# Four high tiles for staging, two running-sum tiles with separate carries, logits behind the next rows' transposes, and epsilon as a third column

## The reference, cut to what matters

```python
# x (8, 2048, 512)
h = layernorm(x) * (1 + ca) + sa
xn = layernorm(h) * ln_gamma + ln_beta
k, v, r = xn @ Wk.T, xn @ Wv.T, xn @ Wr.T
kv = k * v
csum = cumsum(kv * sigmoid(time_decay) ** t, axis=time)        # over 2048 rows of a batch
wkv = sigmoid(time_first) * kv + sigmoid(time_decay) * shifted(csum)
x = x + ga * ((sigmoid(r) * wkv) @ Wo.T)
h = layernorm(x) * (1 + cb) + sb
# two groups of 32 experts, the best 2 of each group for every row
logits = h @ router_w                     # (rows, 64)
x = x + gb * mean over the two groups of the weighted SwiGLU experts of h
```

## Time and profile before

| | |
|---|---|
| median of the runs | 4927.58 us (3 runs, 4915.73 to 4927.71) |
| the profiled execution | 4905.73 us, its span 4904.0 us |
| share of the span busy | PE 93%, PEld 77%, DVE 63%, ACT 34%, POOL 58% |
| mean granted TensorE clock | 0.971 |
| stage A in the trace | from about 78 to about 1905 us |

### The profile page before, as it was taken

One profiled execution on the slowest core, in us unless ns is written; L12 is line 12 of the kernel. 1 busy time (PEld: TensorE's weight loads), 2 busy tenths in 40 slices (PEclk: granted clock), 3 DMA queues, 4 the chain that ended last, 5 costly groups with the idle time before them and its releaser, 6 DMA issues.

```text
span 4904.0 us, 89177 instructions
## 1 busy us (share of the span) xinstructions
PE 4580.8 (93%) x22649; PEld 3764.6 (77%) x22649; DVE 3080.2 (63%) x6077; ACT 1651.2 (34%) x4093; POOL 2858.1 (58%) x2300
## 2 busy tenths in 40 slices
PE   6999999999999995889999998999999999999998
PEld 4877777777777774667777777888788888888887
DVE  5999999999999996444444444444344444444443
ACT  2444444444444442222222222332222222222222
POOL 2577777777777776445444454555455555555554
PEclk8999999999999997899999999999999999999999
DMA  6767666666666674889899989998998988988887
GB/s 240 234 200 228 195 222 196 214 200 220 207 200 227 196 226 159 261 271 285 252 279 280 280 238 270 294 278 223 290 239 222 260 221 242 258 231 221 220 222 195
DMA packets 434624, 1152.46 MB, mean 235 GB/s; under 512 B 59361, under 2 KB 59362, under 8 KB 415666
## 3 DMA queue, kind: packets, MB, share of 16 engines
q0 software_dynamic: 182512, 454.27, 39.3%
q1 hardware_dynamic: 231106, 619.79, 36.6%
q10 hardware_dynamic: 20736, 75.51, 4.2%
HBM read 719.35 MB, written 463.57 MB: 241 GB/s over the span
## 4 chain that ended last, share of the span: by engine, by line
PE 42%; DMA 12%; issue 4%; POOL 2%; DVE 1%; POOLq 0%; SPq 0%; ACT 0%; DVEq 0%
PE ps L1316 12%; PE ps L1318 12%; PE ps L1317 12%; DMA out<-c_yo,c_idx 11%; PE ps L1325 4%; PE ps L1344 2%; POOL out L1307 1%; POOL c_xg L1274 1%; DMA c_wt<-wsp_d 0%; POOLq L1299 0%; DVE c_yo L1571 0%; POOL list_d L1279 0%; DMA list_d<-pairs,sidx 0%; DMA c_lists<-list_d,c_rowu 0%; DVE c_xl L1559 0%
## 5 line engine op out<-in xcount | busy, mean ns | idle before, releaser
L1307 POOL DMA_INDIRECT out<-c_yo,c_idx x576 | 915.1, 1589 | 933.9 <-DMA out<-c_yo,c_idx 512.5
L1316 PE MATMUL ps<-c_wt,c_xh 128*128 128x512 f32 x2304 | 964.1, 418 | 24.9 <-issue 16.8
L1318 PE MATMUL ps<-c_wt,c_xl 128*128 128x512 f32 x2304 | 910.3, 395 | 0.0
L1317 PE MATMUL ps<-c_wt,c_xh 128*128 128x512 f32 x2304 | 904.0, 392 | 0.0
L1274 POOL DMA_INDIRECT c_xg<-h2g_d,c_idx x576 | 565.0, 981 | 507.6 <-DVE c_yo L1571 400.5
L1555 DVE TENSOR_TENSOR c_hh<-ps,c_sil 128x256 f32<-128x256 f32 x576 | 244.2, 424 | 913.5 <-ACT c_sil L1398 843.5
L1571 DVE SCALAR_TENSOR_TENSOR c_yo<-ps,c_wc,c_xg 128x512 f32<-128x512 f32 x576 | 432.3, 750 | 529.2 <-PE ps L1318 261.5
L442 PE MATMUL ps<-xTh,wTh 128*128 128x512 f32 x1536 | 625.9, 407 | 53.5 <-DVE xTl L818 46.9
L1403 ACT CAST c_xh<-ps 128x512 fp32r<-128x512 f32 x576 | 339.2, 589 | 962.2 <-PE ps L1325 874.2
L709 POOL DMA_INDIRECT list_d<-pairs,sidx x496 | 545.5, 1100 | 188.5 <-issue 123.9
L1398 ACT ACTIVATE c_sil<-ps 128x256 f32<-128x256 f32 x576 | 221.3, 384 | 1177.1 <-PE ps L1318 1105.3
(11 more groups left out here) (199 smaller groups left out, 7776.2 us busy)
## 6 DMA issues: line engine op xcount, KB each, us to landing
c_wt<-wsp_d SPq DMA_DIRECT2D x69, 2048.0 KB
sraw<-wex SPq DMA_DIRECT2D x290, 256.0 KB
wsp_d<-shigh SPq DMA_DIRECT2D x288, 256.0 KB
wsp_d<-sraw SPq DMA_DIRECT2D x288, 256.0 KB
c_wt<-wsp_d SPq DMA_DIRECT2D x69, 1024.0 KB
xin<-x SPq DMA_DIRECT2D x34, 1024.0 KB
h2g_d<-mod_d SPq DMA_DIRECT2D x128, 256.0 KB
out<-xin SPq DMA_DIRECT2D x32, 1024.0 KB
```

Source lines behind the costliest of these rows:

```text
L1307: nc.gpsimd.indirect_dma_start(out=out, out_offset=bass.IndirectOffsetOnAxis(ap=idx[:, n:n + 1], axis=0), in_=yo[:, n % 4, :], in_offset=N ...
L1316: nc.tensor.matmul(o, lh, rh, start=first, stop=False)
L1317: nc.tensor.matmul(o, lh, rl, start=False, stop=False)
L1318: return nc.tensor.matmul(o, ll, rh, start=False, stop=last)
```

## The change

Five edits, all in stage A:

- `shigh` has four tiles. `stage_hi` writes to `shigh[j % 4]` and waits no longer for the store of job j - 2; the stores count on four semaphores rather than two. SP still waits for the stores of job j - 4 before it loads job j.
- `cs` has two tiles rather than four, used by chunk parity. The carries live in `cr`, one column for each chunk. `hi` on ACT copies the last column of the running sum into `cr` ahead of its cast, and DVE's carry copies from `cr`. DVE's carry also waits for `carried` of two chunks before, and for `wkv_ready` of two chunks before.
- On PE, `project(3)` is done in one piece, then `front`, then `logits`. The groups are numbered anew: v and r of chunk 3 are 19 and 20, `front` 21 to 24, the logits 25.
- On ACT, the copy of the logits goes to the very end of the step, behind `hi` 3.
- The tiles of mean and variance get a third column that holds epsilon; the `tensor_scalar` that added it (L781, L807, L859) becomes a `tensor_reduce` over columns 1 and 2.

```diff
-PROJ = ((0, 1, 2), (8, 9, 10), (11, 12, 13), (18, 20, 21))
-OUTP, RANK, BACKT, LOGIT, FRONTT = 3, 7, 14, 19, 22
+PROJ = ((0, 1, 2), (8, 9, 10), (11, 12, 13), (18, 19, 20))
+OUTP, RANK, BACKT, FRONTT, LOGIT = 3, 7, 14, 21, 25
...
-        cs = sb("cs", [P, KC, TT + 1])
+        cs = sb("cs", [P, 2, TT + 1])
+        cr = sb("cr", [P, KC])
...
-        shigh = sb("shigh", [P, 2, C], F32R)
+        shigh = sb("shigh", [P, 4, C], F32R)
...
             def stage_in(b, j):
...
-                gate(sp, (low_of(j - 4), lows(b, j - 4)), (stg_out[j % 2], jout(b, j - 4)))
+                gate(sp, (low_of(j - 4), lows(b, j - 4)), (stg_out[j % 4], jout(b, j - 4)))
...
-                project(b, s, 3, (0,))
+                project(b, s, 3)
+                front(b, s)
                 if not (first and s == 0):
                     logits(b, s)
-                project(b, s, 3, (1, 2))
-                front(b, s)
...
             def hi(b, s, dc):
                 act.wait_ge(s_ready, cnt(b, s, 4, dc + 1))
+                wait(act, carry, cnt(b, s, 4, dc + 1))
+                nc.scalar.copy(cr[:, dc:dc + 1], cs[:, dc % 2, TT:TT + 1]).then_inc(carried, 1)
                 wait(act, out_done, cnt(b, s - 1, 4, 4))
...
-                    wait(act, stg_out[j % 2], jout(b, j - 2))
-                    dst = shigh[:, j % 2]
+                    dst = shigh[:, j % 4]
...
                 stage_hi(b, at + 7)
-                if back_too:
-                    logits(b, s)
                 stage_hi(b, at + 8)
                 stage_hi(b, at + 9)
                 front(b, s, (0, 1))
                 chunk_r(b, s, 3)
                 front(b, s, (2, 3))
                 hi(b, s, 3)
+                if back_too:
+                    logits(b, s)
...
-                    V.tensor_scalar(vaf[:], mvf[:, :, 1], EPS, None, ALU.add).then_inc(f_var, 1)
+                    V.tensor_reduce(vaf[:], mvf[:, :, 1:3], AX_X, ALU.add).then_inc(f_var, 1)
...
-                    V.tensor_scalar(vag[:], mvg[:, :, 1], EPS, None, ALU.add).then_inc(g_var, 1)
+                    V.tensor_reduce(vag[:], mvg[:, :, 1:3], AX_X, ALU.add).then_inc(g_var, 1)
...
-                wait(dve, wkv_ready, cnt(b, s - 1, 4, dc + 1))
+                wait(dve, wkv_ready, cnt(b, s, 4, dc - 1))
+                wait(dve, carried, cnt(b, s, 4, dc - 1))
                 if s == 0:
-                    V.memset(cs[:, dc, 0:1], 0.0).then_inc(carry, 1)
+                    V.memset(cs[:, dc % 2, 0:1], 0.0).then_inc(carry, 1)
                 else:
-                    V.tensor_copy(cs[:, dc, 0:1], cs[:, dc, TT:TT + 1]).then_inc(carry, 1)
+                    V.tensor_copy(cs[:, dc % 2, 0:1], cr[:, dc:dc + 1]).then_inc(carry, 1)
...
-                V.tensor_scalar(vab[:], mvb[:, :, 1], EPS, None, ALU.add).then_inc(b_var, 1)
+                V.tensor_reduce(vab[:], mvb[:, :, 1:3], AX_X, ALU.add).then_inc(b_var, 1)
```

More of the change, by code:

```diff
@@ L108, in jout @@
     row, at = (0, j) if j >= 0 else (-1, j + JOBS)
-    n = row * (SPLITS // 2) + sum(i not in WO_PART for i in range(at % 2, at + 1, 2))
+    n = row * (SPLITS // 4) + sum(i not in WO_PART for i in range(at % 4, at + 1, 4))
     if isinstance(b, int):
-        return (b * (SPLITS // 2) + n) * 32
-    return b * (SPLITS // 2 * 32) + n * 32
+        return (b * (SPLITS // 4) + n) * 32
+    return b * (SPLITS // 4 * 32) + n * 32
 def lows(b, j):
@@ L235, in stage_a @@
         stg_in = [sem(f"stg_in{i}") for i in range(4)]
-        stg_out = [sem("stg_out0"), sem("stg_out1")]
+        stg_out = [sem(f"stg_out{i}") for i in range(4)]
         scattered = [sem("scattered0"), sem("scattered1")]
@@ L264, in stage_a @@
         kv_ready, carry, wk_ready, scan = sem("kv_ready"), sem("carry"), sem("wk_ready"), sem("scan")
+        carried = sem("carried")
         wkv_ready = sem("wkv_ready")
@@ L284, in worked @@
             if n < 0:
-                return n == -1 and q >= FRONTT
+                return n == -1 and FRONTT <= q < FRONTT + KC
             behind = 2 if q == RANK else 1 if OUTP <= q < RANK or BACKT <= q < BACKT + KC or q == LOGIT else 0
@@ L355, in stage_out @@
                     _, _, rows, part = split_at(b, j)
-                    for col, tile in zip(PARTS[part], (shigh[:, j % 2].bitcast(F32), sraw[:, j % 4])):
-                        sp.dma_start(wsp_d[rows, col:col + C], tile).then_inc(stg_out[j % 2], 16)
+                    for col, tile in zip(PARTS[part], (shigh[:, j % 4].bitcast(F32), sraw[:, j % 4])):
+                        sp.dma_start(wsp_d[rows, col:col + C], tile).then_inc(stg_out[j % 4], 16)
             def stage_in(b, j):
@@ L427, in _ @@
             sp.wait_ge(gb_out, 16 * 16 * B)
-            for par in range(2):
-                sp.wait_ge(stg_out[par], 32 * SPLITS // 2 * B)
+            for i in range(4):
+                sp.wait_ge(stg_out[i], 32 * SPLITS // 4 * B)
             for par in range(2):
@@ L689, in stage_lo @@
                 else:
-                    dst, high = sraw[:, j % 4].bitcast(F32R), shigh[:, j % 2]
+                    dst, high = sraw[:, j % 4].bitcast(F32R), shigh[:, j % 4]
                 nc.gpsimd.tensor_tensor(dst, sraw[:, j % 4], high.bitcast(F32), ALU.subtract).then_inc(low_pool, 1)
@@ L836, in chunk @@
                 dve.wait_ge(carry, cnt(b, s, 4, dc + 1))
-                V.tensor_tensor_scan(cs[:, dc, 1:TT + 1], ones[:, 0:1].to_broadcast([P, TT]), wk,
-                                     cs[:, dc, 0:1], ALU.mult, ALU.add).then_inc(scan, 1)
+                V.tensor_tensor_scan(cs[:, dc % 2, 1:TT + 1], ones[:, 0:1].to_broadcast([P, TT]), wk,
+                                     cs[:, dc % 2, 0:1], ALU.mult, ALU.add).then_inc(scan, 1)
                 dve.wait_ge(scan, cnt(b, s, 4, dc + 1))
                 V.scalar_tensor_tensor(out=aa[:, dc % 2, :], in0=kv, scalar=tfc[:, dc:dc + 1],
-                                       in1=cs[:, dc, 0:TT], op0=ALU.mult, op1=ALU.add).then_inc(wkv_ready, 1)
+                                       in1=cs[:, dc % 2, 0:TT], op0=ALU.mult, op1=ALU.add).then_inc(wkv_ready, 1)
             def residual(b, s):
@@ L1036, in _ @@
             g.memset(half[:], -0.5)
+            for t in (A["mvf"], A["mvg"], A["mvb"]):
+                g.memset(t[:, :, 2:3], EPS)
             g.memset(hit[:], 0.0)
@@ L1130, in _ @@
                 else:
-                    sign, size = cs[0:B, 1, 0:C], cs[0:B, 2, 0:C]
+                    sign, size = cs[0:B, 1, 0:C], sg[0:B, 1, 0:C]
                     link(V.tensor_scalar(size, p, -1.0, None, ALU.mult))
```

12 lines of the change are left out of this document (6 added, 6 removed).

## The result

The changed kernel takes 4853.0 us (median of 4 runs, 4845.5 to 4860.0), the kernel before 4924.3 beside it: a ratio of 0.9858 with a 95% interval of 0.9837 to 0.9879, so 1.4% faster. The forecast was 4848. Its profiled execution took 4859.97 us at a span of 4858.2, against 4905.73 before. That pair is only 46 us apart, where the medians are 71 apart. The other 15 have no place in the traces: the profiled execution of before was faster than each of its four timed runs, that of the changed kernel the slowest of its four.

A forecast was written before the change was run, and what follows sets the result against it. DVE paces stage A, with PE's 52.7 us a step close under it. Gains of 41.7 + 16.3 + 20 + 13.5 = 91.5 us, less 2 and 10, leave 80: 4848 us against the median 4927.6, range 4803 to 4898.

The forecast's parts named there:

- Epsilon, size and mechanism: DVE's three epsilon additions in stage A: POOL holds them; as reductions they run unheld, 41.7 us kept.
- Does the stall just move?: DVE behind the epsilon additions: only L859's 7.0 us moves, to L811; the other 41.7 us are gained.
- Its L882 waits 16.3 us; these go: DVE's low part of staging: its 16.3 us of waits for ACT, 9 cases, vanish with four high tiles.
- The waits for ACT: DVE at L882 and L818: four high tiles take off 16.3 us and 20 of 29.1 us.
- The wait for v: DVE's wait for PE's v of chunk 3, 13.5 us in 14 cases, goes once the logits move.
- The moved logits fill PE's gap before `project(0)`: PE at a step's end: logits behind the transposes fill its 46.9 us of waits, as far as DVE allows.
- PE's floor before a border: Step before a batch border: DVE needs about 51.5 us, PE's 52.7 takes over, so 10 us are lost again.
- The stalls come back: Rival, 0.18: half of epsilon's 41.7 us returns elsewhere on DVE, loads replace half the store waits; 4890 us.
- PE's floor: Rival, 0.12: holds on L795 and the like shrink too, steps reach 52.7 plus about 0.2 us; 4810 us.
- Nothing moves: Rival, 0.07: DVE is held at another meeting, `modulate` or the residual, mid-step; time stays at 4928 us.
- Slower: Rival, 0.05: the logits' copy behind ACT's last cast comes too late for DVE's L890; 4972 us.
- a fixed sum: Easiest way to fail: DVE's stalls with POOL have a total that no single instruction's form can change.

The follow-up runs named there:

- the last kernel above: Changed kernel with job 6's `stage_lo` and `nmg` later, and job 9's cast and low part behind the rest of the step's end: ratio 0.9867 to the kernel before.
- the last four kernels: Changed kernel with job 6's `stage_lo` later: 0.9889; POOL's products apart: 0.9895; `stage_lo` and `nmg` later: 0.9864; these two and job 9's staging last: 0.9867.
- `stage_lo` 6 later: Changed kernel with DVE's low part of staging job 6 moved behind `norm_front(b, s + 2, 0)`: ratio 0.9889 to the kernel before, 31 steps 1708.4 us.

## Why the prediction was right, and where it wasn't

**Epsilon, size and mechanism: right.** Reductions of 161 ns, none held. L859's stall moved to L811 as foretold, 7.0 us against 8.0 measured. Net 49.3 - 8.0 = 41.3 us for 41.7. Alone it lowered DVE's busy time by 41.9.

**"Does the stall just move?": right.** The answer given was no, but for L859's. L820 and `residual` took nothing, and with epsilon alone L882 (1390 ns on the mean for 1379) and L795 (1320 for 1319) stayed as they were.

**"Its L882 waits 16.3 us; these go": right as a wait, mis-sized as a gain.** The wait fell by 15.0 us, but the same instruction was then held by POOL for 12.4 us more, and this came with the high tiles and not with epsilon. L797 took 4.1 us more; what from is open, as its mean is 1320 ns with either of the two parts undone. The sum had nothing for these 16.5 us.

**The waits for ACT: right.** 16.3 to 1.3 us where 0 was forecast, 29.1 to 7.9 where 9 was. No wait of ACT for a store is left; the one for loads, 121.4 us with 4.4 at the longest, took its place. DVE paid for it when it came earlier and the load did not, 85.3 and 83.9 us in the two kernels with `stage_lo` later.

**The wait for v: right, 13.5 to 2.7**, and shown by the kernel with the logits undone, where 13.7 stood again.

**"The moved logits fill PE's gap before `project(0)`": this step failed.** PE's 46.9 us fell to 16.8, not under 10, and with the logits in their old place they were 14.9. So that gap went because DVE's low half came earlier, by the other two parts. With the move by itself it was longer, 55.2 (a likely reason, not tried by itself: PE comes to `project(0)` sooner, and DVE doesn't). What the move brings is the v of chunk 3 and no more, by the difference of the ratios 11 us, near the 13.5 of the sum but within the noise. The 46.9 us were no term of the sum, so this step failed without changing the forecast.

**PE's floor before a border: the sum was near, the border was off.** The plain steps came to 53 to 54 us as forecast. The border's step was to be under 58 and the one shown took 60.5. What is left there is "issue": PE has 10.7 us of it in 3 cases, DVE 17.7 before L791 and 9.7 before L885. L791's six cases are the six times that the loop over `b` starts again, and PE's three fall on three of these; L885's four lie elsewhere. "Issue" is an idle time for which the trace shows no semaphore. The prediction went by waits with a named releaser and left it out, though DVE had 14.9 us of it before L789 and 4.6 before L882 even then. It is now 7.9 us more on DVE. PE's 10.7 are new in the list, but before, DVE's late low half ended PE's wait at every border (4.25 us at 1430), and such time may have lain hidden behind it. What causes it was not tried.

**The total.** 80 us were forecast and 57 measured in stage A. The 16.5 by holds and the 7.9 by issue come near the missing 23, but this is bookkeeping and no proof: the 10 us that the sum took off for PE's floor have no row of their own, and 7 us of the ledger lie in small groups. Against the median the forecast was 80 off 4927.6; the measured difference of the medians is 71 us, and the interval of the ratio allows 59 to 80. So the execution that stage A was compared in makes the miss look larger than the ratio does, and the single traces can't settle which is nearer. That 4848 came within 5 us of 4853.0 is in part luck: the medians differ by 14 us more than stage A does.

**The rivals.** "The stalls come back" came near in size, 16.5 of its 21 us, but not by its mechanism, half of the epsilon stalls: 12.4 of them came with the high tiles. Its other half, the loads in the place of the stores, didn't come. "PE's floor" (4810) was not reached; only the plain steps of the last kernel above stand at it. "Nothing moves" is excluded by the interval. "Slower" did not show: L893 waited for the logits' copy 0.6 us in all steps; its 11.2 us behind the last step were 12.0 before. The warning that DVE's stalls could be a fixed sum is answered: with the two-input form the form decides, so it isn't fixed; but three of the last four kernels show how holds and waits replace each other: DVE's busy time went from 1622.6 to 1565.2, 1617.5 and 1560.8 us and the 31 steps stayed at 1701 to 1710.

## What to carry to other kernels

Where several causes of delay end at one meeting (here POOL's hold, ACT's queue and a late v, all ahead of PE's `project(0)`), removing one mostly lengthens the next: two parts that brought 0.32% and 0.16% alone brought 1.2% together, so a part should be judged by taking it out of the full set as well as by adding it alone. Look at what the next load waits for before moving the line that frees its tile. Read busy time as suspiciously as idle time: compare the shortest and the mean of each form, since a hold by another engine is booked as work. And look at "issue" before the first instructions of a loop's body, which no named releaser accounts for.

## What the runs showed of the hardware

POOL's products over SBUF tiles held even DVE instructions of four numbers in each partition: at the place of L781 these took 883 to 1806 ns on the mean as `tensor_scalar` (3582 at the longest in the kernel before), 1685 with two SBUF inputs, and 161 ns as a reduction, although POOL's products ran beside each of these reductions. L820, which reads one of its two inputs from PSUM, wasn't held either: 693 ns at the longest in 128 cases of the changed kernel, all but one beside a product of POOL. Two products back to back kept DVE out for the length of both (2.99 us in the rows above). POOL's issuing of its indirect list transfers didn't: in the same rows DVE's instruction ended while such an issue (1269.96 to 1271.22) was under way, and in the kernel with `stage_lo` 6 later L885 took its unheld 0.68 us at 1266.24 while one ran from 1266.13 to 1267.75.
